# Causal masks and softmax divisions moved to GpSimd, with query-major scores in two-bank PSUM tiles and key-major scores in two single banks

## What is computed

```python
x = x + attn_a(layernorm(x))   # 16 query heads, one shared key head and one value head, causal
x = x + ffn(layernorm(x))      # shared SwiGLU of 1024 columns + top 2 of 8 routed experts
x = x + attn_b(layernorm(x))   # 16 heads with own keys and values, ALiBi bias, causal
x = x + ffn(layernorm(x))      # the same weights again
```

## Time and profile before

| | before |
|---|---|
| median of 3 runs | 1174.56 us (1174.39 to 1176.03) |
| profiled execution | 1174.42 us, span 1172.5 us |
| PE busy | 1062.2 us, 91% of the span |
| DVE busy | 815.1 us, 70% |
| ACT busy | 593.8 us, 51% |
| POOL busy | 280.7 us, 24% |
| mean granted TensorE clock | 0.961 |

### The profile page before, as it was taken

One profiled execution on the slowest core, in us unless ns is written; L12 is line 12 of the kernel. 1 busy time (PEld: TensorE's weight loads), 2 busy tenths in 40 slices (PEclk: granted clock), 3 DMA queues, 4 the chain that ended last, 5 costly groups with the idle time before them and its releaser, 6 DMA issues. The chain is left out here.

```text
span 1172.5 us, 20784 instructions
## 1 busy us (share of the span) xinstructions
PE 1062.2 (91%) x7296; PEld 682.5 (58%) x7296; DVE 815.1 (70%) x1632; ACT 593.8 (51%) x1256; POOL 280.7 (24%) x270
## 2 busy tenths in 40 slices
PE   4789999999986798999987999999999868989998
PEld 3434444444455687888875344444434556878887
DVE  6897888888255854447787988888883657554475
ACT  6316667767642234543353366666776322445432
POOL 3450000000026024525753000000000351155270
PEclk9859999999997999999998799999999979999999
DMA  4540111110025124633249412222200431246343
GB/s 130 148 77 12 39 33 35 39 38 12 12 62 177 46 73 121 154 101 117 72 134 179 78 45 59 54 59 60 64 12 12 131 113 41 69 130 150 109 142 100
DMA packets 59237, 95.02 MB, mean 81 GB/s; under 512 B 14431, under 2 KB 43039, under 8 KB 56785
## 3 DMA queue, kind: packets, MB, share of 16 engines
q1 hardware_dynamic: 38405, 52.28, 17.3%
q10 hardware_dynamic: 13820, 22.54, 6.8%
q0 software_dynamic: 6912, 18.88, 6.3%
HBM read 66.33 MB, written 26.67 MB: 79 GB/s over the span
## 5 line engine op out<-in xcount | busy, mean ns | idle before, releaser
L1124 ACT ACTIVATE pt<-st_ps 128x512 f32<-128x512 f32 (+3 forms) x768 | 332.8, 493 | 207.9 <-PE st_ps L779 92.6
L776 PE MATMUL st_ps<-qs,ks 99*128 99x512 bf16 (+7 forms) x768 | 244.4, 329 | 7.5 <-ACT pt L1124 5.7
L1347 DVE TENSOR_REDUCE mab<-su_ps 128x1 f32<-128x512 f32 (+2 forms) x288 | 182.3, 660 | 21.9 <-PE su_ps L756 13.4
L792 PE MATMUL o_ps<-pt,vp 128*32 128x512 f32 (+3 forms) x1536 | 163.2, 498 | 0.0
L752 PE MATMUL su_ps<-ks,qs 96*128 96x512 bf16 (+5 forms) x448 | 159.8, 371 | 3.3 <-DVE mab L1347 2.4
L776 PEld LDWEIGHTS st_ps<-qs,ks 99*128 99x128 bf16 (+1 forms) x768 | 74.7, 98 | 105.5 <-ACT pt L1124 50.5
L557 POOL TENSOR_SCALAR ve<-mv 128x4 f32<-128x4 f32 x16 | 5.4, 338 | 538.9 <-DVE mv L1256 538.9
L614 POOL DMA_INDIRECT rows_in<-rows,source x80 | 77.8, 972 | 170.2 <-PE st_ps L959 84.7
L1148 ACT CAST hh<-hf 128x512 fp32r<-128x512 f32 x64 | 39.7, 620 | 148.2 <-DVE hf L1551 148.2
L779 PE MATMUL st_ps<-cstb 128*128 128x128 bf16 x512 | 111.5, 220 | 0.0
L164 PE MATMUL st_ps<-xt_h,wu 128*128 128x512 f32 x256 | 101.7, 397 | 5.0 <-DVE hf L1551 2.0
(11 more groups left out here) (220 smaller groups left out, 2144.2 us busy)
## 6 DMA issues: line engine op xcount, KB each, us to landing
wu_raw<-w_units_dram SPq DMA_DIRECT2D x32, 384.0 KB, 3.2
outs<-rows_out ACTq DMA_DIRECT2D x40, 256.0 KB, 2.2
qs<-q_parts ACTq DMA_DIRECT2D x60, 128.0 KB
q_parts<-hml SPq DMA_DIRECT2D x16, 384.0 KB, 2.7
wexp_raw<-w_units_dram SPq DMA_DIRECT2D x16, 384.0 KB, 6.5
qs<-q_parts SPq DMA_DIRECT2D x36, 128.0 KB
inv<-inverses SPq DMA_DIRECT2D x128, 32.0 KB, 1.9
rows<-xn SPq DMA_DIRECT2D x8, 512.0 KB, 4.9
```

The lines of the kernel that those rows point to most:

```text
L776: last = pe.matmul(bank[KM_BANKS[n % len(KM_BANKS)]][:, lo - CH * part:hi - CH * part], key_stack(l, s)(j)[0:rows, P * kt:P * kt + P], qs[ ...
L792: last = pe.matmul(o_ps[32 * j:32 * j + 32, lo:hi], vp[:, QT * b + kt, 4 * g + j if l else 4 * (g % 2), :], pt[:, kt % 2, j, lo:hi], start ...
L1124: act.activation(pt[:, kt % 2, j, lo:hi], bank[KM_BANKS[i % len(KM_BANKS)]][:, lo - CH * part:hi - CH * part], ACT.Exp, scale=1 / np.sqrt( ...
L1347: dve.tensor_reduce(to, bank[SU_BANKS[n % len(SU_BANKS)]][:, 0:share * width].rearrange("p (j k) -> p j k", j=share), AX.X, ALU.max).then_ ...
```

## The change

The key-major masks go. In the first attention's 8 steps and in 6 of the second's 8 (`masks_after`), POOL sets the exponentials above the diagonal to zero in `pt` (`affine_select` over 128 x 4 x 128, one per diagonal quad), and `values` waits for that. In steps 0 and 4 of the second attention PE masks as before. POOL also takes all divisions but those of each attention's last step, and `add_bias` and two `rstds` are put among its masks. Key-major pieces have two single banks, and query-major scores two tiles of two banks: 20 units of up to 1024 columns in place of 38. The sums are gathered on 128 partitions in place of 32.

```diff
-KM_BANKS = (0, 1, 2)
-SU_BANKS = (3, 6, 7)
+KM_BANKS = (0, 1)
+SU_TILES = 2
...
-            units += [(qt, 0, j, 1, CH, False) for j in range(4)]
+            units += [(qt, 0, j, 2, CH, False) for j in (0, 2)]
         width = P * (qt % HALF + 1)
-        share = min(4, CH // width)
+        share = 4 if 4 * width <= N else 2
...
-INVERT_AT, DIVIDE_AT = (3, 21), (14, 34)
+INVERT_AT, DIVIDE_BEHIND = (3, 13), (2, 6)
...
+def masks_after(l, s):
+
+    return l == 0 or s % G > 0
...
-        sums = sb("sums", [32, 2, 2, CH // 8], F32)
+        sums = sb("sums", [P, 2, 2, CH // 32], F32)
...
-        su_ps = [ctx.enter_context(nc.psum_tensor(f"su_ps{n}", [P, CH], F32)) for n in range(2)]
+        su_ps = ctx.enter_context(nc.psum_tensor("su_ps", [P, N], F32))
...
+        su_tile = [st_ps[1], su_ps]
...
+            def mask_exponentials(l, s):
+
+                S = step_no(l, s)
+                for q in range(len(QUADS)):
+                    kt, _ = QUADS[q]
+                    lo, _ = queries(q)
+                    if lo == P * kt:
+                        if masks_after(l, s):
+                            block = pt[:, kt % 2, :, lo:lo + P]
+                            pool.wait_ge(p_ready, PIECES * S + 4 * q + 4)
+                            pool.affine_select(block, block, [[0, 4], [1, P]], ALU.is_ge, 0.0, base=0, channel_multiplier=-1).then_inc(masked, 1)
+                        if S == 1:
+                            add_bias(2 * kt, 2 * kt + 2)
+                        if s == STEPS - 1 and kt == ROOTS_AT:
+                            rstds(2 * l + 1, 0, 1)
+                        if s and kt in DIVIDE_BEHIND:
+                            divide(l, s - 1, DIVIDE_BEHIND.index(kt))
+
+            def divide(l, s, part):
+                b, g = divmod(s, G)
+                n0 = N * b + CH * part
+                half = slice(CH * part, CH * part + CH)
+                pool.wait_ge(inv_in, 64 * (2 * step_no(l, s) + part + 1))
+                own = ot[:, g // 2, n0:n0 + CH]
+                if g % 2 == 0:
+                    pool.tensor_tensor(own, ou[:, half], inv[:, 0, half], ALU.mult).then_inc(ot_done, 1)
...
             def feed_forward(f):
-                rstds(2 * f + 1, 0, 2)
+                rstds(2 * f + 1, 1, 2)
...
-                out_b = bank[SU_BANKS[n % len(SU_BANKS)]]
-                wait(pe, su_used, n - len(SU_BANKS) + 1)
+                out_b = su_tile[n % SU_TILES]
+                wait(pe, su_used, n - SU_TILES + 1)
...
-                diagonal = lo == P * kt
+                diagonal = lo == P * kt and not masks_after(l, s)
...
+                lo, hi = queries(q)
+                if lo == P * kt and masks_after(l, s):
+                    pe.wait_ge(masked, QT * mask_turn(l, s) + kt + 1)
                 pe.wait_ge(p_ready, PIECES * S + 4 * q + 4)
...
                 invert(step_no(l, STEPS - 2), 0)
-                divide(l, STEPS - 2, 0)
                 invert(step_no(l, STEPS - 2), 1)
...
                 stats(p, 0)
-                divide(l, STEPS - 2, 1)
                 normalise(p, 0)
...
                 normalise(p, 1)
                 invert(step_no(l, STEPS - 1), 0)
-                divide(l, STEPS - 1, 0)
+                divide_last(l, 0)
```

More of the change, by code:

```diff
@@ L40 @@
 GBUFS = 8
+ROOTS_AT = 3
 RPAIRS = 4
@@ L83, with apart @@
 NSU = len(SU) + 1
+def apart(share, width):
+    return width if share * width <= CH or CH % width == 0 else CH
 QUADS = [(kt, part) for kt in range(QT) for part in range(kt // HALF, 2)]
@@ L152, in turns, with mask_turn @@
     return (l and len(range(s % SBANKS, STEPS, SBANKS))), s // SBANKS + 1
+def masks_after(l, s):
+    return l == 0 or s % G > 0
+def mask_turn(l, s):
+    return sum(masks_after(*divmod(n, STEPS)) for n in range(STEPS * l + s))
 def wait(eng, sem, count):
@@ L346, in qkv_bank @@
             first = NCH * len(QKV[0])
-            return bank[4 + n % 4] if n < first else bank[(n - first) % 3]
+            if n < first:
+                return bank[4 + n % 4]
+            return bank[(n - first) % (2 if n >= qkv_index(1, NCH - 1, 2) else 3)]
         def tr_bank(p, c, k):
@@ L571, in zero_inverses, with add_bias @@
                 pool.memset(inv[:, :, :], 0.0).then_inc(inv_zeroed, 1)
-            def add_bias():
+            def mask_exponentials(l, s):
[22 more added lines that the diff above has]
+                    pool.tensor_tensor(own, ou[:, half], inv[:, 0, half], ALU.mult).then_inc(ot_done, 1)
+                else:
+                    n = 2 * ((STEPS // 2 - 1) * l + s // 2) + part
+                    pool.tensor_tensor(ou[:, half], ou[:, half], inv[:, 1, half], ALU.mult).then_inc(spread_done, 1)
+                    pool.wait_ge(spread_done, n + 1)
+                    pool.tensor_tensor(own, own, ou[:, half], ALU.add).then_inc(ot_done, 1)
+            def add_bias(first, end):
                 pool.wait_ge(wfc_in, 32)
-                for t in range(TT):
+                for t in range(first, end):
                     pool.wait_ge(xn_done, t + 1)
@@ L647, in _ @@
             pool.wait_ge(qkv_done, NCH * len(QKV[0]))
+            mask_exponentials(0, 0)
             split_weights(2, wp_h[:, :, :], wp_l[:, :, :], 768)
-            add_bias()
+            for s in range(1, STEPS):
+                mask_exponentials(0, s)
             feed_forward(0)
@@ L657, in _ @@
             zero_inverses(1)
+            for s in range(STEPS):
+                mask_exponentials(1, s)
             feed_forward(1)
@@ L682, in qkv_group @@
                 if l:
-                    wait(pe, evac_done, n - 2 if n >= qkv_index(1, 0, 3) else 0)
+                    if n >= qkv_index(1, NCH - 1, 2):
+                        pe.wait_ge(evac_done, n - 1)
+                    elif n >= qkv_index(1, 0, 3):
+                        pe.wait_ge(evac_done, n - 2)
                 else:
@@ L1346, in maximum @@
                     to = mab[:, S % 2, half, j0:j0 + share, qt - HALF]
-                dve.tensor_reduce(to, bank[SU_BANKS[n % len(SU_BANKS)]][:, 0:share * width].rearrange("p (j k) -> p j k", j=share),
+                step = apart(share, width)
+                dve.tensor_reduce(to, su_tile[n % SU_TILES][:, 0:share * step].rearrange("p (j k) -> p j k", j=share)[:, :, 0:width],
                                   AX.X, ALU.max).then_inc(su_used, 1)
@@ L1357, in maxima_parts @@
                 dve.wait_ge(su_ready, n + 1)
-                src = bank[SU_BANKS[n % len(SU_BANKS)]][0:32, 0:P]
+                src = su_tile[n % SU_TILES][0:32, 0:P]
                 dve.tensor_scalar(nmx[:, a, 0, :], src, -1.0, None, ALU.mult).then_inc(nm_step, 1)
@@ L1369, in invert, with divide_last @@
                 dve.reciprocal(sums[:, 1, part, :], sums[:, 0, part, :]).then_inc(inv_done, 1)
-            def divide(l, s, part):
-                b, g = divmod(s, G)
-                n0 = N * b + CH * part
+            def divide_last(l, part):
+                n0 = N * (NB - 1) + CH * part
                 half = slice(CH * part, CH * part + CH)
-                dve.wait_ge(inv_in, 64 * (2 * step_no(l, s) + part + 1))
-                own = ot[:, g // 2, n0:n0 + CH]
-                if g % 2 == 0:
-                    dve.tensor_tensor(own, ou[:, half], inv[:, 0, half], ALU.mult).then_inc(ot_done, 1)
-                else:
-                    n = 2 * (STEPS // 2 * l + s // 2) + part
-                    dve.tensor_tensor(ou[:, half], ou[:, half], inv[:, 1, half], ALU.mult).then_inc(odd_done, 1)
-                    dve.wait_ge(odd_done, n + 1)
-                    dve.tensor_tensor(own, own, ou[:, half], ALU.add).then_inc(ot_done, 1)
+                S = step_no(l, STEPS - 1)
+                dve.wait_ge(inv_in, 64 * (2 * S + part + 1))
+                dve.wait_ge(ot_done, 2 * S)
+                own = ot[:, G // 2 - 1, n0:n0 + CH]
+                dve.tensor_tensor(ou[:, half], ou[:, half], inv[:, 1, half], ALU.mult).then_inc(odd_done, 1)
+                dve.wait_ge(odd_done, 2 * l + part + 1)
+                dve.tensor_tensor(own, own, ou[:, half], ALU.add).then_inc(ot_done, 1)
             def attention(l):
@@ L1396, in attention @@
                                     invert(step_no(l, s - 1), part)
-                                if s and u == DIVIDE_AT[part]:
-                                    divide(l, s - 1, part)
                             maximum(l, s + 1, u)
@@ L1434, in between @@
                 normalise(p, 2)
-                divide(l, STEPS - 1, 1)
+                divide_last(l, 1)
                 add_projection(l, 6)
```

15 lines of the change are left out of this document (8 added, 7 removed).

## The result

The changed kernel takes 1248.16 us (median of 4 runs, 1247.42 to 1249.98) where the kernel before took 1174.47 (4 runs, 1174.31 to 1176.03): a ratio of 1.0627, 95% interval 1.0608 to 1.0645. It is slower by 73.7 us, where the sum gave 60.5. The profiled span is 1245.6 us against 1172.5.

What follows compares the result with a forecast made beforehand. The prediction took PE's own work to bound the kernel. Steps +19.7 and +20.8, last steps +6.8, behind the attentions +15.8 and openings -2.6 made +60.5 us on 1174.42: about 1234 us, range 1190 to 1250.

Steps and rivals of the forecast that it cites:

- the sum: All terms added to the profiled 1174.42 us: steps, last steps, stretches behind attentions and openings, together +60.5, about 1234 us.
- the late root: Behind each attention, chunk 1's root queues on POOL behind the last mask and delays the projection: +7.9 us each, 15.8 together.
- Steps of 34.0 us: Attention steps with units: 28.4 us of PE work, 3.2 of waits at q0 to q8, 2.4 at q9 to q11.
- the 0.9 of waits: PE's waits in a step before the change, for DVE above all; 0.9 us that may go whole.
- POOL's prices: On POOL a mask takes 0.8 us, a division 1.3 or 2.6 for odd groups; nothing counted for them within both ends.
- The rival of a slow mask: POOL's mask is slow: 1262 us in all at 3 us a mask, 1375 at 5; chance 0.05.
- 1.3 counted: At each attention's opening DVE works through the first units without cover, so fewer reductions save 1.3 us.
- 5 x 34.0 + 2 x 35.9: Attention 2's seven steps, two of them keeping masks on PE, against 221.0 us before: +20.8 us.
- +3.4 us each: Each attention's last step, which has no units and whose projection tiles fill only some gaps: 3.4 us longer.
- the rival given 0.02: The clock falls as PE waits in each step: a tenth of 16 steps at 1.2 GHz adds 45 us, 1280; chance 0.02.
- the ring costs half: The two-bank ring's waits cost 2.8 us a step, giving steps of 31.2 and about 1192 us; chance 0.19.
- PE's work alone bounds: Two banks cost nothing, steps take 28.4 + 0.4 = 28.8 us and the kernel 1137 to 1153; chance 0.10.

Runs made afterwards that it cites:

- the keys on SP: The changed kernel with attention 2's transfers of key stacks and slopes issued by SyncE instead of ScalarE: 1240.42 us, ratio 1.0587.
- three banks: The changed kernel with three key-major banks and 38 single-bank units as before, masks and divisions on POOL, chunk 1's root late: 1164.95 us, ratio 0.9931.
- three banks and the root early: The changed kernel with three key-major banks, 38 single-bank units and chunk 1's root behind key tile 4's mask in each last step: 1149.55 us, ratio 0.9799.
- Two banks alone: The kernel before with one line changed, key-major pieces on two banks instead of three: 1226.42 us, ratio 1.0453.
- the one with the early root: The changed kernel with only chunk 1's root moved, from behind the last mask to behind key tile 4's mask: 1230.03 us, ratio 1.0468.
- the filler: The changed kernel with 18 extra unused matmuls in each attention, in steps 6 and 7: 1247.62 us, ratio 1.0621.
- moved units: The changed kernel with its query-major units grouped behind other pieces, their number and size unchanged: 1245.8 us, ratio 1.0607.

## Why the prediction was right, and where it was off

The direction and the range held: 1248 lies in 1190 to 1250, 2 us from its end, and some 13 us above the sum. The mechanisms were the ones named, but that the total stayed inside the range is partly luck. The issues on ACT (5.3 us) and the clock were in no term; with the keys on SP attention 1, with the same code, had a full clock and took 238.66 and 35.23 us for its seven steps and the last, where the profile of the changed kernel has 241.12 and 38.68 and the sum 238.0 and 34.9. Against that, the stretch between the attentions came out 3 us shorter than counted.

The runs split the 74 us as follows, by their ratios and for a kernel before of 1174 us: POOL's masks and divisions with three banks and the root early, 23.6 less; the late root, 15.5 more; two key-major banks for three, 56.6 more; two-bank units, 25.1 more. Each is good to some 2 to 5 us. By the steps of the prediction:

- **Steps of 34.0 us: right, 34.24.** Against three banks, the changed quads q0 to q7 are 0.14, 0.50, 0.47, 0.37, 0.25, 0.45, 0.41 and 0.03 us longer, 2.6 in all, where the count had 2.4; q8 has 0.56 (0.75 counted). The values of q8 to q10 came within 0.14 us of their counted places: from those of q7 to those of q10 9.19 us pass, 2.5 more than the 6.67 of work (2.4 counted). So the step holds as work and waits, 28.4 + 5.8 us. It does not hold as a difference from three banks. There a step takes 29.65 us and not the 28.4 + 0.4 of the rival, for it waits too, 0.8 us of it between those same values (7.50 us), and the two rings of the change cost 4.6 us on top, not 5.6. Half of the 3.7 us of masks on PE was to go and all of the 0.9 of waits; q0, q2, q4 and q6 did get 0.23 us shorter each, four masks of 0.058, but q8 to q11 together only 0.35 where 16 masks were taken out. The exponentials of q9 to q11 wait for values before and after the earlier trace rows, which is the likely reason. With three banks seven steps went from 218.27 to 208.59 us, 1.4 us a step, half of the 2.8 from 31.2 to 28.4.
- **POOL's prices: right.** The mask takes 635 ns, nearer the cast than the 0.8 taken, a division 1.27 us, and nothing waits for them in a step. The rival of a slow mask is excluded by that row, which is near the one-input cast. The Trainium skill's about 12 cycles an element (GPSIMD Engine Reference, Elementwise side-by-side cycle accounting) would have made it 5.1 us; its tight loop, 768 ns, is the nearer, and the measured mask is shorter than even that.
- **The late root: right**, 15.4 and 18.7 us by the two pairs of kernels for the predicted 15.8. The stretch between the attentions rose by only 3.5, for 6.6 counted. In it the projection came 7.3 us later, but from attention 2's first unit (660.77) to its first piece 32.15 us passed where 34.36 had (from 627.33), 2.2 less for 1.3 counted; the other 1.6 us less are not placed. Two banks alone, which keeps the 38 reductions, takes 31.7 us there, so it is not shown that the fewer reductions gave the gain. Behind attention 2 the 9.3 us for 7.9 go with 33.2 us at the low clock, where the kernel before and the one with the early root have 20.5.
- **The second attention: a term too small by 5.8 us.** "5 x 34.0 + 2 x 35.9" took its steps as the first attention's. ACT's issues of key stacks and slopes between exponentials were not counted; moving them took 5.3 us off seven steps.
- **The last steps: "+3.4 us each"** measured 3.7 at full clock (35.23, keys on SP) and 4.2 with the filler's own work in it (35.70). In the profile of the changed kernel they are 7.2 and 6.0, with 10.7 and 6.8 us at 1.2 GHz.
- **The clock: the rival given 0.02 came partly true.** "A tenth of the 16 steps at 1.2 GHz" was far too much, but the whole span has 132.2 us at 1.2 GHz where it had 92.2. In the steady steps it stayed at 1.00. The row that spoke against the rival (331.50 to 352.00) was not read there but just behind attention 1, and in that place it did not carry over: in the changed kernel the clock fell in the last step and again from 359.1 to 362.5 and 365.9 to 372.7 us. The Trainium skill (TensorE: Matmul & The Clock Gate, A second HAM failure mode: psum-queue depth-cycling) tells of a kernel in which PE idled between groups as it cycled through PSUM banks, until the clock swung. That is not borne out in the steps with their two-bank ring, where the clock stayed at 1.00 with PE idle 2.65 of 34.20 us.

The rivals fell so: "the ring costs half" by the step of 34.24; "PE's work alone bounds" by the same, and even without the ring it was 12 us too low at either end (1149.55 with the root early and 1164.95 with it late, for its 1137 and 1153), as steps took 29.65 and not 28.8 us.

## What to carry to other kernels

Count a PSUM ring from rows, as start of the matmul to start of the consumer, the consumer's duration, and its end to the next start; quad by quad that count was within 0.2 us here. Do not use it to promise a gain from another order: it promised 2.3 us a step for moved units, and none came. Moving work to an idle engine was worth 24 us here, but only with the third bank kept and with nothing short and urgent queued behind that engine's last long wait. When a fall of the clock is filled with dummy work, look at the stretches that follow before believing in the gain. Before transfers go to another queue, look at what stands behind them there.
